# Weight sums made in DRAM by adding DMAs; weight halves made for the first token pair only

## What is computed

```
h = silu(x @ w_gate) * (x @ w_up)                 # 2048 tokens x 2048
h_sparse = keep the 2 largest |h| of each 4       # along the 2048
x = layernorm(x + h_sparse @ w_down)
```

## Time and profile before

| | us |
|---|---|
| median of 3 runs | 1158.88 |
| lowest, highest | 1153.5, 1162.85 |
| the profiled execution | 1152.48 |
| its span | 1150.7 |
| TensorE busy (matmul) | 1023.0 (89%) |
| VectorE busy | 888.2 (77%) |
| ScalarE, GpSimd busy | 605.0 (53%), 536.5 (47%) |
| mean granted TensorE clock | 0.961 |

### The profile page before, as it was taken

The page is one execution under the profiler, slowest core; times in us unless marked ns, Lnnn a source line. Parts: engine busy times, 40 slices in busy tenths (PEclk is TensorE's granted clock), DMA queues, the critical chain, the costliest instruction groups (busy, mean ns, idle before and its releaser), DMA issues.

```text
span 1150.7 us, 18114 instructions
## 1 busy us (share of the span) xinstructions
PE 1023.0 (89%) x5830; PEld 817.5 (71%) x5831; DVE 888.2 (77%) x1889; ACT 605.0 (53%) x1141; POOL 536.5 (47%) x640
## 2 busy tenths in 40 slices
PE   7989999998999769999986998889959989899886
PEld 6667777776777648788775876767747767678665
DVE  5898799688778865665759486675988889777894
ACT  5787588578758952234364323453543423544424
POOL 2194457347445613223457355563443557445224
PEclk9999999999999989999998998999979989899998
DMA  8877277356716632233321332221201212103001
GB/s 265 247 203 183 85 194 219 102 180 175 193 59 175 212 109 65 75 121 135 101 74 37 38 73 37 8 67 37 74 3 34 74 37 91 51 14 101 18 20 73
DMA packets 61081, 116.78 MB, mean 101 GB/s; under 512 B 6976, under 2 KB 9024, under 8 KB 60992
## 3 DMA queue, kind: packets, MB, share of 16 engines
q1 hardware_dynamic: 56112, 101.48, 32.2%
q0 software_dynamic: 4880, 14.18, 3.2%
HBM read 84.69 MB, written 30.94 MB: 100 GB/s over the span
## 4 chain that ended last, share of the span: by engine, by line
PE 34%; DVE 13%; ACT 5%; DMA 5%; issue 4%; POOL 2%; SPq 1%; POOLq 0%; DVEq 0%; ACTq 0%
PE f_bank L53 20%; PE f_bank L1955 12%; DVE h_lo L2356 4%; DMA w_raw<-gate 3%; ACT h_hi L2120 2%; DMA wd_raw<-down 2%; DVE beats L2323 2%; ACT w_hi L2047 1%; DVE h L2347 1%; PE f_bank L1829 1%; ACT wd_hi L2055 1%; DVE h L2299 1%; ACT h L2102 1%; PE f_bank L1837 1%; DVE x_lo_T L2267 1%
## 5 line engine op out<-in xcount | busy, mean ns | idle before, releaser
L53 PE MATMUL f_bank<-wd_hi,h_hi 128*128 128x512 f32 x256 | 109.0, 426 | 48.8 <-DVE h_lo L2356 43.4
L714 ACT ACTIVATE probs<-bank,nmax 128x384 f32<-128x384 f32 (+3 forms) x256 | 131.7, 549 | 21.4 <-DVE nmax L899 19.2
L883 DVE CUSTOM_DVE_ANT_0 bank<-bank,mask 128x384 f32<-128x384 f32 (+3 forms) x256 | 123.0, 502 | 13.7 <-PE bank L510 12.8
L521 PE MATMUL bank<-ident,probs 128*128 128x128 f32 x640 | 108.7, 284 | 24.5 <-DVE pt_lo L908 11.1
L908 DVE TENSOR_TENSOR pt_lo<-bank,pt_hi 128x512 f16<-128x512 f32 (+1 forms) x192 | 114.8, 598 | 16.7 <-ACT pt_hi L724 16.3
L2097 ACT ACTIVATE h<-f_bank 128x512 f32<-128x512 f32 x64 | 37.4, 596 | 165.1 <-PE f_bank L1955 163.7
L724 ACT ACTIVATE pt_hi<-bank 128x512 f16<-128x512 f32 (+1 forms) x192 | 104.9, 546 | 23.4 <-PE bank L521 22.9
L1740 POOL TENSOR_TENSOR w_lo<-w_raw,w_hi 128x512 fp32r<-128x512 f32 x48 | 82.7, 1738 | 63.4 <-ACT w_hi L2047 63.3
L1955 PE MATMUL f_bank<-x_hi_T,w_hi 128*128 128x512 f32 x256 | 101.4, 396 | 6.7 <-ACT h L2097 2.7
L53 PE MATMUL f_bank<-wd_lo,h_hi 128*128 128x512 f32 x256 | 106.5, 416 | 0.0
L53 PE MATMUL bank<-x_hi,w_qk 128*128 128x512 f32 x256 | 100.7, 412 | 6.2 <-DVE x_lo L913 5.7
(11 more groups left out here) (275 smaller groups left out, 2928.1 us busy)
## 6 DMA issues: line engine op xcount, KB each, us to landing
big_lo<-q_hi_dram SPq DMA_DIRECT2D x32, 256.0 KB
big_lo<-q_lo_dram SPq DMA_DIRECT2D x32, 256.0 KB
big_lo<-k_hi_dram SPq DMA_DIRECT2D x32, 256.0 KB, 3.7
big_lo<-k_lo_dram SPq DMA_DIRECT2D x32, 256.0 KB, 5.2
w_raw<-up SPq DMA_DIRECT2D x32, 256.0 KB, 3.6
w_raw<-gate SPq DMA_DIRECT2D x32, 256.0 KB, 4.5
wd_raw<-down SPq DMA_DIRECT2D x32, 256.0 KB, 3.9
rows<-sorted_dram SPq DMA_DIRECT2D x19, 256.0 KB, 2.6
```

What stands on the lines that cost most here:

```text
L53: ins = pe.matmul(out, a(k, i), b(k, j), start=(n == 0), stop=(n == len(chain) - 1))
L521: ins = pe.transpose(TP[u % TR][:, j * P:(j + 1) * P], probs[u % RP][:, j * P:(j + 1) * P], ident[:, :])
L714: ins = act.activation(probs[u % RP][:, at:at + cols(r)], S[u % SR][:, at:at + cols(r)], ACT.Exp, bias=nmax[:, r, c:c + 1])
L883: dve.tensor_tensor_reduce(out=S[u % SR][:, at:at + cols(r)], in0=S[u % SR][:, at:at + cols(r)], in1=mask[:, T - cols(r):T], scale=1.0, sc ...
```

## The change

The host lays gate and up out by halves (`by_half`), one unit of 256 KB per round and half. At the start of the expert stage SyncE copies up, up, gate, gate halves (four copies of 2 MB) into `sums_dram`. GpSimd then issues 16 DMAs of 512 KB that add to it in DRAM: four for the first two units (steps 0, 2, 4), twelve for the others (steps 6, 7, 9, 12), each with a wait for those before. `weight_sums` is gone. Signs are changed so that each sum is an addition.

The raw weight buffer now lies on the lo buffer, so the lo is made in place, and the load of weight X of the next round waits for this round's product of X (and for its stores). In rounds 0 to 7 SyncE also stores hi and lo of each weight to `kept_dram` (14 stores of 256 KB a round). In rounds 8 to 15 it loads both back in place of the raw weights (14 loads), and nothing is split.

ScalarE copies product 1 into bank FB, product 2 is accumulated on it there, and SiLU reads the bank with scale -1; the "11" adds are gone. `kept_hi` moves ahead of the copies of product 7; `kept_lo` moves into `early`, and in even rounds the whole chain L-1 now stands in `early`. Magnitudes use three buffers in turn.

```
+    FREED = ("1", "6", "5", "7", "2", "4", "3")
...
+    LO_ON_POOL = ("6", "7", "4")
+    LO_ON_DVE = ("1", "5", "2", "3")
...
-raw = at("w_raw", [P, 2, 2048], F32, ring)
-aw = [at(f"w_{h}", [P, GROUPS, 2, HALF * P], F32R, ring + 16 * KB + 14 * KB * n) for n, h in enumerate(("hi", "lo"))]
+aw = [at(f"w_{h}", [P, NPR, HALF * P], F32R, ring + 16 * KB + 14 * KB * n) for n, h in enumerate(("hi", "lo"))]
+raw = at("w_raw", [P, NPR, HALF * P], F32, ring + 30 * KB)
...
+MADE = 2 * NCH
+COPIED = 16 * 4
+SUMMED = (16 * 4, 16 * 16)
...
+    return d % 3
...
+def wraw_count(n):
+    return 16 * (n // RW + 1) + 16 * max(0, (n - n % RW + RW - NW * 2 * NCH) // RW)
+def weight_source(L, X):
+    u = L % (2 * NCH)
+    return {"1": gate[0, u], "2": gate[1, u], "4": up[1, u], "5": sums_dram[0, u], "7": sums_dram[1, u],
+            "6": sums_dram[2, u], "3": sums_dram[3, u]}[X].rearrange("p (i n) -> p i n", i=2)
...
+    def weight_in(L, X):
+        n = weight(L, X)
+        if X in "5673":
+            sp.wait_ge(s_order, SUMMED[L > 1])
+        if n >= RW:
+            sp.wait_ge(s_wraw[n % RW], wraw_count(n - RW))
         if L > 0:
-            sp.wait_ge(*wlo_ready(L - 1, GROUPS - 1))
-            sp.wait_ge(*wlo_ready(L - 1, GROUPS - 2))
+            sp.wait_ge(s_pr, product_done(L - 1, X + "b"))
+        if 0 < L <= 2 * NCH:
+            sp.wait_ge(s_wst[(n - NW) % 2], 32 * ((n - NW) // 2 + 1))
+        if L >= 2 * NCH:
+            for i in range(2):
+                sp.dma_start(both(aw[i], X).bitcast(F32),
+                             kept_dram[i, L - 2 * NCH, FREED.index(X)].rearrange("p (i n) -> p i n", i=2)).then_inc(s_wraw[n % RW], 16)
+            return
+        sp.dma_start(both(raw, X), weight_source(L, X)).then_inc(s_wraw[n % RW], 16)
+    def weight_out(L, X):
+        n = weight(L, X)
+        if n >= 2:
+            sp.wait_ge(s_wst[n % 2], 32 * (n // 2))
+        sp.wait_ge(*wlo_ready(L, X))
         for i in range(2):
-            j = 2 * (L % 2) + i
-            sp.dma_start(raw[:, i, 0:4 * P], up[chunk(L), j]).then_inc(s_wraw, 16)
-            sp.dma_start(raw[:, i, 4 * P:8 * P], gate[chunk(L), j]).then_inc(s_wraw, 16)
+            sp.dma_start(kept_dram[i, L, FREED.index(X)].rearrange("p (i n) -> p i n", i=2),
+                         both(aw[i], X).bitcast(F32)).then_inc(s_wst[n % 2], 16)
...
+            if n == EARLY:
+                weight_in(0, FREED[0])
+            if EARLY <= n < EARLY + NW - 1:
+                weight_in(0, FREED[n - EARLY + 1])
...
-    weights_in(0)
+    for n, of in enumerate((up[0], up[0], gate[0], gate[1])):
+        sp.dma_start(sums_dram[n].rearrange("u p n -> (u p) n"),
+                     of.rearrange("u p n -> (u p) n")).then_inc(s_draw, 16)
...
+    for L in range(1, ROUNDS):
+        for X in FREED:
+            store_until(weight(L, X) - 3)
+            weight_in(L, X)
+        if L == 1:
+            block_in(3)
+            down_in(0)
+        if L >= 4 and L % 2 == 0:
+            down_in(L // 2 - 1)
...
+    def sum_weights(at, of, units, waits):
+        wait_apart(pool, s_passed, waits)
+        for u in units:
+            pool.dma_start(sums_dram[at, u:u + 2].rearrange("u p n -> (u p) n"),
+                           of[u:u + 2].rearrange("u p n -> (u p) n"), accum_op=ALU.add,
+                           max_dma_last_dim=8192).then_inc(s_order, 16)
+    FIRST, OTHERS = (0,), (2, 4, 6)
+    sums_at = {0: ((0, up[1], FIRST, [(s_draw, COPIED)]), (1, gate[0], FIRST, [(s_draw, COPIED)])),
+               2: ((2, sums_dram[0], FIRST, [(s_order, 32)]),),
+               4: ((3, sums_dram[2], FIRST, [(s_order, 48)]),),
+               6: ((0, up[1], OTHERS, [(s_order, SUMMED[0])]),),
+               7: ((1, gate[0], OTHERS, [(s_order, SUMMED[0])]),),
+               9: ((2, sums_dram[0], OTHERS, [(s_order, SUMMED[0] + 96)]),),
+               12: ((3, sums_dram[2], OTHERS, [(s_order, SUMMED[0] + 144)]),)}
...
-        if n == 2:
-            weight_sums(0)
-        if n in first_group and first_group[n] % 2 == 1:
-            weight_lo(0, first_group[n])
+        for sum_of in sums_at.get(n, ()):
+            sum_weights(*sum_of)
+        if n in first_weight and first_weight[n] in LO_ON_POOL:
+            weight_lo(0, first_weight[n])
...
-        if L + 1 < ROUNDS:
-            weight_sums(L + 1)
         if L >= 2 and L % 2 == 0:
             down_lo((L - 2) // 2)
-        if L + 1 < ROUNDS:
-            for g in range(1, GROUPS, 2):
-                weight_lo(L + 1, g)
+        if L + 1 < MADE:
+            for X in FREED:
+                if X in LO_ON_POOL:
+                    weight_lo(L + 1, X)
...
-        if AT[name] % 2 == 0:
-            pe.wait_ge(*wlo_ready(L, AT[name] // 2))
+        if name[1] == "a":
+            if L < MADE:
+                pe.wait_ge(*wlo_ready(L, which))
+            else:
+                pe.wait_ge(s_wraw[weight(L, which) % RW], wraw_count(weight(L, which)))
...
             to = FB
-            if name == "2b":
-                pe.wait_ge(s_ad, added(L, "11a"))
-            elif L > 0:
-                pe.wait_ge(s_ad, added(L - 1, "11b"))
+            pe.wait_ge(s_cp, copied(L, "1" + name[1]))
...
+    def weight_hi(L, X):
+        n = weight(L, X)
+        act.wait_ge(s_wraw[n % RW], wraw_count(n))
+        act.activation(both(aw[0], X), both(raw, X), ACT.Copy).then_inc(s_whi, 1)
...
+        if name == "1b":
+            act.wait_ge(s_silu, NS + 4 * L + 1)
+        elif name == "1a" and L > 0:
+            act.wait_ge(s_silu, NS + 4 * (L - 1) + 2)
+        to = FB[:, :] if name[0] == "1" else {"6": us, "7": hv[hslot[L, 1]]}[name[0]][:, i, :]
+        act.activation(to, VB[i][:, :], ACT.Copy).then_inc(s_cp, 1)
...
-        act.activation(x, x, ACT.Silu).then_inc(s_silu, 1)
+        if r == 0:
+            act.wait_ge(s_pr, product_done(L, "2" + "ab"[i]))
+            if L == 0 and i == 0:
+                act.wait_ge(s_y, NS)
+            x, of = hv[hslot[L, 0]][:, i, :], FB[:, :]
+        else:
+            act.wait_ge(s_ad, added(L, "12" + "ab"[i]))
+            x = of = us[:, i, :]
+        act.activation(x, of, ACT.Silu, scale=-1.0).then_inc(s_silu, 1)
...
-        more = L + 1 < ROUNDS
-        soon = L >= 3 and odd and more
+        more = L + 1 < MADE
         copy(L, "1a")
-        copy(L, "1b")
-        if L == 0:
-            token_hi(0, "T4")
-            token_hi(0, "B22")
         if L == LB + 1:
             token_hi(1, "T3")
             token_hi(1, "T4")
...
         elif L > 0 and L != LB + 1:
             magnitudes(s - 1, 1, 0)
             magnitudes(s - 1, 1, 1)
+        silu(L, 0, 0)
+        copy(L, "1b")
+        if L == 0:
+            token_hi(0, "T4")
+            token_hi(0, "B22")
         copy(L, "6a")
         copy(L, "6b")
-        if soon:
-            weight_hi(L + 1, 0)
-            weight_hi(L + 1, 1)
+        if more:
+            weight_hi(L + 1, "1")
+        if L >= 2 and L != LB + 1:
+            kept_hi(L - 2)
+        copy(L, "7a")
+        copy(L, "7b")
+        if L == LB + 1:
+            kept_hi(L - 2)
         if L >= 2 and not odd:
             down_hi(s - 1, range(2))
-        copy(L, "7a")
-        copy(L, "7b")
-        silu(L, 0, 0)
-        if L >= 2:
-            kept_hi(L - 2)
+        silu(L, 0, 1)
+        for X in ("6", "5") if more else ():
+            weight_hi(L + 1, X)
         if L >= 2 and not odd:
             down_hi(s - 1, range(2, J))
         if L == LB + 1:
             magnitudes(s - 1, 1, 0)
             magnitudes(s - 1, 1, 1)
-        for g in range(2 if soon else 0, 4) if more else ():
-            weight_hi(L + 1, g)
-        silu(L, 0, 1)
-        for g in (4, 5) if more else ():
-            weight_hi(L + 1, g)
...
+        for X in ("7", "2", "4") if more else ():
+            weight_hi(L + 1, X)
...
+        if more:
+            weight_hi(L + 1, "3")
...
-        if L == LB + 1:
-            compare(L - 2)
-            count_first(L - 2)
-            count_second(L - 2)
-            choose(L - 2)
-        elif L >= 2 and L % 2 == 0:
-            compare(L - 1)
+        if L >= 2 and L % 2 == 0:
+            chain = L - 1 if L != LB + 1 else L - 2
+            compare(chain)
+            count_first(chain)
+            count_second(chain)
+            choose(chain)
+        if L >= 2 and L != LB + 1:
+            kept_lo(L - 2)
...
+        ways = (compare, count_first, count_second, choose) if L % 2 == 1 or L == LB + 1 else ()
         if adds:
             add_up(d, 0)
-        if L > 0:
-            count_first(chain)
+        for way in ways[:2]:
+            way(L - 1)
...
-        more = L + 1 < ROUNDS
+        more = L + 1 < MADE
         if L == 0:
-            weight_lo(0, GROUPS - 1)
             token_lo(0, "T3")
-        add_product(L, "11a")
-        if L == 0:
             token_lo(0, "T4")
             token_lo(0, "B22")
         if L == LB + 1:
...
             token_lo(1, "T4")
             token_lo(1, "B22")
         early(L)
```

(30 more changed lines are left out.)

225 lines of the change are left out of this document (93 added, 132 removed).

## The result

| | before | after |
|---|---|---|
| median of five runs, us | 1158.9 | 1166.6 |
| lowest, highest | 1152.7, 1162.9 | 1165.5, 1169.6 |
| span of the profiled execution | 1150.7 | 1163.9 |
| mean granted clock | 0.961 | 0.954 |
| expert stage, us | 126.1 | 151.3 |

The ratio is 1.008, with an interval of 1.0052 to 1.0109: the changed kernel is 0.8% slower. The forecast was 1144, 1.3% faster. The time lies in the range given and within 1% of no change, on the other side of it than forecast.

The account below looks back on a forecast made before the run. TensorE was taken to bound both stages. Feed-forward -34 us (waits -22.8, clock -13, late loads +2) and expert stage +19 gave -15 from the 1158.9 us median: 1144 us, range 1109 to 1186.

Parts of the forecast that it names:

- Part 1: Feed-forward stage: moving `kept_lo` ahead removes all TensorE waits for `h_lo` but round 8's; gain up to 43.4 us.
- Part 2: Feed-forward stage: VectorE's chain is late next; TensorE idles 50.6 us against 73.4, so -22.8 us.
- The list of new waits by rounds: Feed-forward stage: TensorE's new idle time, listed for rounds 0 to 15 and the end, summed to 50.6 us.
- Part 3: Feed-forward stage: removed sums, adds and splitting gain nothing further; ScalarE's new order costs 0 (0 to +1.5 us a round).
- Part 4: Feed-forward stage: loads land late beside GpSimd's scatters in rounds 2 to 5, weight 2 tightest; +2 us (0 to +20).
- The clock term: Feed-forward stage: fewer long waits, so 12 of 25 us lost to the lower clock stay; -13 us (0 to -25).
- Part 5: Expert stage: copies in DRAM delay row 3's transposes 14 us and tile 1's `y` 18 us; +19 us in all.
- The adding: Expert stage: the adding DMAs cost +2 us for issue (0 to +20).
- the estimate from the Trainium skill: Expert stage: 358 GB/s counted for reads and writes makes the copies 47 us, the stage +32, the whole -2.
- rival 1: Expert stage: DRAM sums hold it, copies +35 us and slow adding DMAs stopping GpSimd at step 9; 1180 us, chance 0.21.
- rival 2: Feed-forward stage: VectorE's chain stays at contended length, or weights load late; feed-forward -12 us, total 1166, chance 0.24.
- second branch: Feed-forward stage: the alternative within rival 2, that the late weights of part 4 add their 20 us.

Follow-up runs that it names:

- chain_split: Changed kernel with order scatters in rounds 7 to 10, copy 1a first, and the chain of rounds 2, 4 and 6 divided as before; 1118.2 us, ratio 0.9602.

## Why the prediction was wrong

**The bound** was right: both stages are TensorE's, and every loss is a wait of TensorE or its clock.

**Part 1, `kept_lo`: right.** All `h_lo` waits but round 8's went, and alone this is worth 3.1%, more than the whole forecast.

**Part 2, the chain: right in the second pair, too small in the first.** Forecast 0.7 in rounds 10, 12 and 14: measured 0.55 in each. Forecast 9 in round 2: 7.9. Forecast 5 in rounds 4 and 6: none shown, because a longer wait stands in front, and 8.3 and 7.6 once that is away. I put 2 us on GpSimd's lo of the weights beside the chain and nothing on its `down_lo`, beside which `choose` takes 4.7 to 5.8 us instead of 2.49, and `kept_lo` 4.5 instead of 3.4. Round 8: 4 forecast, 6.7 (5.96 and 0.77). The list of new waits by rounds adds up to 49.6 us, not 50.6; nothing hangs on that.

**Part 3, ScalarE's new order, costed at 0 (0 to +1.5 a round): wrong, the first failed step.** I counted the slack of the "11" path within a round from 4.8 us on, and not what stands ahead of copy 1a on ScalarE from the round before: the last hi of seven, whose load can only start when product 3 is done. In round 0 it is T3's hi, which waits 3.81 us for a token sum of VectorE. The three waits cost 19.1 us, of which my sum had 7.0 (2.0, 2.5 and 2.5 for other reasons). Copy 1a first took half of them away.

**Part 4, late loads, +2 (0 to +20): the second failed step.** That loads land late beside the scatters was named, with the earlier trace rows as its row, but I priced a landing of 10 us as if the slack of the kernel before were still there, and I looked for it at the wrong weight: at weight 2, whose lo TensorE needs last. What waited was hi of weight 1, with a load of 17.0 us, and TensorE for the copies of 7 that stand behind it on ScalarE, one round after the rounds named. The waits were 10.45, 11.03 and 1.46, 22.9 us; taking them away uncovered the chain, so the net was 9.9 in the first pair.

**The clock term, -13: mis-sized.** 577.6 - 65.4 - 486.2 - 7 leaves 19 us against 25: -6. The granted clock was 0.89 in the first pair, with its waits of 6 to 11 us, and 0.98 in the second, with waits mostly under 1; in chain_split the first has 0.99. So here long waits and a low clock go together, and more long waits stood than forecast.

Together: idle -8.0 instead of -20.8, clock -6.1 instead of -13, so -14.1 and not -34.

**Part 5, the expert stage, +19: the size nearly right at +25, in part by luck.** Row 3's transposes were forecast 14 us late and were 13.8, but two errors cancel in this. They were due at 439.0 and not at 445.5, which is row 4's line; and the copies, at 281 GB/s instead of 243, brought row 3's load in at 453.9 instead of 459.6. With the right line the forecast's own landing would have made them 20.6 us late. By the estimate from the Trainium skill (HBM Reference, section Specifications), reads and writes together at 358 GB/s, the copies would take 47 us; they took 29.8. So either the two are not to be counted together, or the figure does not bound a core that runs alone as this one does; no run here separates the two. The adding, taken at +2 for its issue, cost some 10 us, through transfers beside it that landed late, not through a second stop at step 9: rival 1 was wrong in its place and its size. Adding DMAs of 512 KB sent three together landed 2.5 to 4.0 us after one another, 131 to 210 GB/s of payload against the copies' 281. The Trainium skill (Collectives: The Full Stack, section The bandwidth ceiling: the fold count and why AG ≠ RS ≠ AR) has half the copy's rate for the adding phase of a collective in a ring of cores. Half of 281 is 140, at the low end of what was measured here within one core's memory, with other transfers beside them. No run here shows the landing of a plain DMA of that size.

**The rivals.** The time is rival 2's, 1166. Its second branch, "or the late weights of part 4 add their 20", happened. So did its first, the chain at contended length, in the first pair only: in round 2 of the changed kernel, and in rounds 4 and 6 once the loads are in time (5.76 and 4.69 us for `choose`). That the time agrees to a microsecond is luck all the same: the rival has -12 and +19, the stages moved by -14.1 and +25.2, and the medians by less than the profiled executions. The late weights had no place of their own in the sum of chances, and they deserved more than a clause.
